# Squared queries split into two bf16 halves, reordered turns, double-buffered weight chunks, and an earlier context transpose in a gated cross-attention + ternary FFN kernel

## What is computed

```python
# x (32, 100, 512); ctx (32, 361, 256); 16 heads of 128; all fp32
h = layernorm(x)
q = rmsnorm((h @ Wq).reshape(B, 100, 16, 128), gq)
k = rmsnorm((ctx @ Wk).reshape(B, 361, 16, 128), gk)
v = (ctx @ Wv).reshape(B, 361, 16, 128)
a = softmax(einsum('bqhd,bkhd->bhqk', q, k) / sqrt(128))
x = x + tanh(g_xattn) * (einsum('bhqk,bkhd->bqhd', a, v).reshape(B, 100, 2048) @ Wo)
x = x + tanh(g_ffn) * bitlinear_ffn(layernorm(x))   # ternary weights, 8-bit activations, 512 -> 2048 -> 512
```

## Time and profile before

| | us |
|---|---|
| median of 3 runs | 2326.5 (2323.11 to 2329.4) |
| the profiled execution | 2321.96 |
| its span | 2320.2 |
| PE busy in the span | 2209.8 (95%) |
| DVE / ACT / POOL busy | 1820.5 / 1612.1 / 1265.4 |
| PE idle, 240 to 1080 us | 8.2 |
| PE idle, 1080 to 1920 us | 19.0 |

### The profile page before, as it was taken

How to read it: one execution, slowest core, us unless ns; L and a number is a source line. 1 busy time by engine, 2 the same in 40 slices (tenths; PEclk the granted TensorE clock), 3 DMA queues, 4 the chain that set the end, 5 groups by cost and what they waited for, 6 DMA issues and landing times. The chain is left out here.

```text
span 2320.2 us, 45840 instructions
## 1 busy us (share of the span) xinstructions
PE 2209.8 (95%) x16338; PEld 1564.2 (67%) x16338; DVE 1820.5 (78%) x4171; ACT 1612.1 (69%) x3398; POOL 1265.4 (55%) x1623
## 2 busy tenths in 40 slices
PE   5799999999999999999999999999999999769999
PEld 3567777777777777777777777776777777524444
DVE  5888877777877777877787787777877777579996
ACT  4677777777776777777777677776777677446665
POOL 4555656565656565656667676766676655200000
PEclk9999999999999999999999999999999999989999
DMA  6777676766767677657776767677767665635655
GB/s 147 172 152 141 127 143 127 141 135 129 141 129 143 130 140 128 136 105 149 136 146 135 154 132 154 132 146 136 137 145 139 132 108 115 177 87 142 140 139 125
DMA packets 921748, 317.53 MB, mean 137 GB/s; under 512 B 864912, under 2 KB 882608, under 8 KB 921264
## 3 DMA queue, kind: packets, MB, share of 16 engines
q1 hardware_dynamic: 921520, 314.61, 67.5%
HBM read 82.09 MB, written 19.40 MB: 44 GB/s over the span
## 5 line engine op out<-in xcount | busy, mean ns | idle before, releaser
L893 DVE TENSOR_TENSOR khat<-keys_ps,krs 128x512 f32<-128x512 f32 (+1 forms) x384 | 263.6, 686 | 286.2 <-POOL krs L1175 286.2
L1181 POOL TENSOR_TENSOR ksplit<-khat,ksplit 128x512 bf16<-128x512 f32 (+1 forms) x384 | 444.6, 1159 | 70.7 <-ACT ksplit L667 68.7
L1175 POOL TENSOR_TENSOR krs<-kvar,minus_half 128x4 f32<-128x4 f32 (+1 forms) x384 | 387.1, 1008 | 32.0
L689 ACT ACTIVATE prob<-score_ps,nbias,qrs 100x361 f32<-100x361 f32 x512 | 329.1, 647 | 65.3 <-DVE nbias L911 63.6
L1172 POOL TENSOR_SCALAR kvar<-kss 128x4 f32<-128x4 f32 (+1 forms) x384 | 88.6, 231 | 513.6 <-DVE kss L883 511.4
L672 ACT ACTIVATE ksq<-keys_ps 128x512 f32<-128x512 f32 (+1 forms) x384 | 228.3, 596 | 196.2 <-PE keys_ps L25 196.2
L923 DVE SCALAR_TENSOR_TENSOR psplit<-prob,rden,psplit 100x361 bf16<-100x361 f32 x512 | 349.3, 690 | 5.5 <-ACT psplit L698 1.4
L698 ACT ACTIVATE psplit<-prob,rden 100x361 bf16<-100x361 f32 x512 | 304.1, 594 | 49.6 <-DVE rden L917 48.7
L23 PE MATMUL keys_ps<-wk_split,ctxT 128*128 128x512 bf16 (+1 forms) x768 | 294.5, 383 | 26.2 <-DMA ctxT<-nat 14.7
L901 DVE TENSOR_REDUCE nmax<-score_ps 100x1 f32<-100x361 f32 x512 | 268.2, 524 | 54.6 <-PE score_ps L25 54.1
L667 ACT ACTIVATE ksplit<-khat 128x512 bf16<-128x512 f32 (+1 forms) x384 | 240.5, 626 | 85.0 <-DVE khat L893 83.7
(11 more groups left out here) (132 smaller groups left out, 5256.7 us busy)
## 6 DMA issues: line engine op xcount, KB each, us to landing
stage<-in_ffn SPq DMA_DIRECT2D x96, 256.0 KB, 3.2
ctx_raw<-in_ctx SPq DMA_DIRECT2D x31, 256.0 KB, 3.4
xin<-in_x SPq DMA_DIRECT2D x32, 200.0 KB
res_rows<-in_x SPq DMA_DIRECT2D x32, 200.0 KB
x_rows<-res_rows SPq DMA_DIRECT2D x32, 200.0 KB
xin<-x_rows SPq DMA_DIRECT2D x25, 256.0 KB, 2.8
xres<-x_rows SPq DMA_DIRECT2D x25, 256.0 KB, 3.0
out<-xres SPq DMA_DIRECT2D x25, 256.0 KB, 2.0
```

Source lines behind the costliest of these rows:

```text
L689: act.activation(prob[:, h, :], score_ps[h % 2][0:SQ, 0:SK], ACT.Exp, bias=nbias[:, b, h:h + 1], scale=qrs[:, v // 2 % 2, r:r + 1], accum_ ...
L893: dve.tensor_tensor(khat[0:KV[t], k, :].rearrange("p (h d) -> p h d", h=G), keys_ps[k][0:KV[t], :].rearrange("p (h d) -> p h d", h=G), rs, ...
L1175: pool.tensor_tensor(krs[0:KV[t], k, :], kvar[0:KV[t], k, :], minus_half[0:KV[t], 0:G], ALU.pow).then_inc(krs_done, 1)
L1181: pool.tensor_tensor(ksplit[0:KV[t], t, 1, :], khat[0:KV[t], (u + t) % 2, :], ksplit[0:KV[t], t, 0, :], ALU.subtract).then_inc(k_lo_done, 1)
```

## The change

- The squares are kept as two bf16 halves in one tile, `qsq_split`: ACT makes the fp32 squares (`queries_square`) of two heads and squares the same PSUM block a second time to bf16 (`queries_square_hi`), POOL subtracts (`query_squares_lo`). `query_squares` then issues 16 bf16 matmuls in place of 8 fp32 ones, with 128 columns of weights each (28 of them padding or a neighbour's), and stands later in PE's list, behind `heads_out` and the third key tile. `queries_lo` waits for both squares too.
- All four lists of `two_turns` have another order.
- Chunks have two buffers in and two out (`w_raw`, `w_out`, all in `stage`, which loses one of its seven load slots); the ternary part's load comes at the end of the turn before, the store one turn after the rounding.
- `ctx_raw` is filled earlier (turn 2 and turn 6 of the pair before), POOL splits it in turns 1 and 3 without a gap, and `turn_ctx` follows `turn_keys` in turns 4 and 5, where it stood ahead of `turn_keys` in turns 5 and 6.

The diff, cut to its core:

```diff
-    OWN_STAGES = 5
+    OWN_STAGES = 4
...
-        qsq = sb("qsq", [P, G, QT], F32)
+        qsq, qsq_split = sb("qsq", [P, TWO, QT], F32), sb("qsq_split", [P, 2 * G * QT + PAD], BF16)
...
-        w_raw, w_out = stage[:, 0, :], sb("w_out", [P, CHUNK], BF16)
+        w_raw, w_out = [stage[:, 0, :], stage[:, 3, :]], [
+            stage[:, 2, k * CHUNK // 2:(k + 1) * CHUNK // 2].bitcast(BF16) for k in range(2)]
...
             def query_squares(i, u):
...
-                eng.wait_ge(q_sq_done, i * (NG * QD) + ((u + 3) // 2 + 1) * QD)
+                eng.wait_ge(q_sqlo_done, i * (NG * QD) + ((u + 3) // 2 + 1) * QD)
                 for b in range(2):
                     for h in range(G):
-                        last = pe.matmul(ps[0:SQ, b * G + h:b * G + h + 1], qsq[:, h, b * SQ:(b + 1) * SQ],
-                                         ones[:, 0:1], start=True, stop=True)
+
+                        out, hi, lo = ps[:, b * G + h:b * G + h + 1], h * QT + b * SQ, (G + h) * QT + b * SQ
+                        pe.matmul(out, qsq_split[:, hi:hi + P], ones[:, 0:1], start=True, stop=False)
+                        last = pe.matmul(out, qsq_split[:, lo:lo + P], ones[:, 0:1], start=False, stop=True)
...
             def queries_square(i, u, k):
...
-                act.activation(qsq[:, k * TWO:(k + 1) * TWO, :],
-                               shared_ps[p][:, 0:TWO * QT].rearrange("p (h q) -> p h q", h=TWO),
-                               ACT.Square).then_inc(q_sq_done, 1)
+                if started(i * (NG * QD) + (u + 3) // 2 * QD + k):
+                    eng.wait_ge(q_sqlo_done, i * (NG * QD) + (u + 3) // 2 * QD + k)
+                act.activation(qsq[:, :, :], ps, ACT.Square).then_inc(q_sq_done, 1)
+
+            def queries_square_hi(i, u, k):
...
+                act.activation(qsq_hi[:, heads, :], ps, ACT.Square).then_inc(q_sqhi_done, 1)
...
+            def query_squares_lo(i, u, k):
...
+                pool.tensor_tensor(qsq_lo[:, heads, :], qsq[:, :, :], qsq_hi[:, heads, :],
+                                   ALU.subtract).then_inc(q_sqlo_done, 1)
```

PE's list in `two_turns` (the others change in the same manner):

```diff
                 if su:
-                    scores(i, u + 1, 0), scores(i, u + 1, 1)
+                    scores(i, u + 1, 0)
+                if qu:
+                    queries(i, u, 1)
                 if ku:
                     keys(i, u + 2, 2)
-                if qu:
-                    queries(i, u, 1)
                 if su:
-                    scores(i, u + 1, 2)
-                mixed(i, u, 0, par)
+                    scores(i, u + 1, 1), scores(i, u + 1, 2)
+                if kv:
+                    keys(i, v + 2, 0)
+                mixed(i, u, 0, par), mixed(i, u, 1, par)
                 if su:
                     scores(i, u + 1, 3)
-                if kv:
-                    keys(i, v + 2, 0)
-                mixed(i, u, 1, par)
                 if kv:
                     keys(i, v + 2, 1)
                 if new_x:
                     turn_x(i, 0)
-                if qu:
-                    query_squares(i, u)
-                if i == TERN_PAIR - 1 and u == 1:
-                    weight_totals(i)
                 heads_out(i, v, 0), heads_out(i, v, 1)
                 if new_x:
                     turn_x(i, 1)
                 if kv:
                     keys(i, v + 2, 2)
+                if qu:
+                    query_squares(i, u)
+                if i == TERN_PAIR - 1 and u == 1:
+                    weight_totals(i)
                 if sv:
                     scores(i, v + 1, 0), scores(i, v + 1, 1)
-                project(i, v, 0), project(i, v, 1)
+                project(i, v, 0), project(i, v, 1), project(i, v, 2), project(i, v, 3)
                 if sv:
-                    scores(i, v + 1, 2)
-                project(i, v, 2), project(i, v, 3)
-                if sv:
-                    scores(i, v + 1, 3)
+                    scores(i, v + 1, 2), scores(i, v + 1, 3)
```

More of the change, by code:

```diff
@@ L76, in shared_uses @@
             if more_queries(u, last):
-                order += [("q", u, 0)]
-            if more_queries(u, last):
-                order += [("q", u, 1)]
+                order += [("q", u, 0), ("q", u, 1)]
             order += [("m", u, 0), ("m", u, 1)]
@@ L82, in shared_uses @@
                 order += [("x", 0)]
-            if more_queries(u, last):
-                order += [("qss", u)]
             order += [("o", v, 0), ("o", v, 1)]
@@ L87, in shared_uses @@
                 order += [("x", 1)]
+            if more_queries(u, last):
+                order += [("qss", u)]
             if has_mixed(v, last):
@@ L386, in load_ternary @@
                 if u == 4:
-                    sp.wait_ge(w_tern_out, MATRICES * CHUNKS * 16)
+                    for k in range(2):
+                        sp.wait_ge(w_tern_out[k], MATRICES * CHUNKS // 2 * 16)
                     sp.wait_ge(shared_done, use(PAIRS - 1, ("q", UNITS - 5, QD - 1))[0] + 1)
@@ L406, in turn @@
                         load_x(i + 1, b, xin, x_in)
-                if not last and u == 3:
-                    sp.wait_ge(nat_ready, (i * 2 + 3) * KVT)
-                    load_ctx(i + 1, 1, ctx_raw)
-                if not last and u in (UNITS - 3, UNITS - 2):
-                    sp.wait_ge(keys_done, tile(i, u + 1, KVT - 1) + 1)
-                    turn_ctx(i + 1, u - (UNITS - 3), 1 - par)
                 if has_keys(u, last):
                     turn_keys(i, u + 2, 0), turn_keys(i, u + 2, 1), turn_keys(i, u + 2, 2)
+                if not last and u in (UNITS - 4, UNITS - 3):
+                    sp.wait_ge(keys_done, tile(i, u + 2, KVT - 1) + 1)
+                    turn_ctx(i + 1, u - (UNITS - 4), 1 - par)
                 load_pieces(i, u, 0)
@@ L421, in turn @@
                 load_pieces(i, u, 2)
+                if not last and u == 2:
+                    sp.wait_ge(nat_ready, (i * 2 + 3) * KVT)
+                    load_ctx(i + 1, 1, ctx_raw)
+                if i < PAIRS - 2 and u == UNITS - 2:
+                    sp.wait_ge(nat_ready, (i * 2 + 4) * KVT)
+                    load_ctx(i + 2, 0, ctx_raw)
                 store_chunk(i, u)
+                load_chunk(i, u, False)
                 if last:
@@ L1204, in split_ctx @@
                     eng.wait_ge(ctx_in[b], (j + 1) * 32)
-                    if not (isinstance(j, int) and j == 0):
-                        eng.wait_ge(shared_done, use(j - 1, ("m", 1, CC - 1))[0] + 1)
+                    if j > 1:
+                        eng.wait_ge(shared_done, use(j - 2, ("m", UNITS - 1, CC - 1))[0] + 1)
                 pool.tensor_copy(nat[0:KV[t], par, b, t, 0, :], raw[0:KV[t], t, :]).then_inc(nat_hi_done, 1)
```

271 lines of the change are left out of this document (156 added, 115 removed).

## The result

| | before | after |
|---|---|---|
| median of the runs, us | 2324.98 (2323.11 to 2329.4, 4 runs) | 2250.82 (2249.86 to 2254.29, 4 runs) |
| profiled execution | 2321.96 | 2254.29 |
| its span | 2320.2 | 2252.5 |
| first turn of `y` (end of pair 0) | 208.7 | 211.4 |
| last turn of `y` | 2030.4 | 1963.3 |

The ratio is 0.9681, 95% interval [0.9663, 0.9699]: 74 us faster, where 40 were forecast, and outside the range of 2262 to 2316.

What follows compares the result with a forecast made beforehand. PE was taken to bound the kernel, busy 2209.8 of 2320.2 us. Squares -36, waits that go -13, waits that come +6 and start +3 gave -40 us, from 2326.5 to 2287 us; range 2262 to 2316.

Steps and rivals of the forecast that it cites:

- The squares: PE's 64 square groups: a load-matmul pair falls from 84 to 49 ns, a group by 0.57 us; -36 us.
- rival C: The squares gain nothing: a fixed 84 ns per one-column matmul, or the chain waits as before; 2322 us, chance 0.09.
- Waits that go: PE's waits for PSUM banks: `qvar` -10, `qT_lo` -3, `xT_lo` and `khat` 0; sum -13 us.
- waits that come: Between second `mixed` and `heads_out`: less cover, so PE waits 0.1 us in each of 60 pairs of turns; +6 us.
- The clock: PE's granted clock was read as full nearly throughout, 2.4 GHz; the sum had no term for it.
- The tie: Ahead of `heads_out`: DVE's subtraction is ready after 1.73 us, against 1.75 us of PE's score and key tile.
- The context's transposes ahead of `turn_probs`: SP's queue in turn 5: three transposes, 4.83 us, covered by later-needed probabilities; 0, bounds 0 to 1 us in 15 pairs.
- The chunks' second buffers: Chunk loads and stores: second buffers take waits off SP's queue, not off PE; 0.
- Start +3: Kernel start: uncovered extra squares on ACT, subtractions on POOL and one load slot fewer; +3 us, ends 0 and 6.
- Drain 0: Kernel end: the 5.3 us wait for `pT` can go either way; 0, bounds ±5 us.
- Rival B: POOL's new subtraction delays DVE's `psplit`, reaching PE 0.86 us each two turns: +53, in sum +13; 2340 us, chance 0.09.
- Rival A: All 27 us of PE's steady idle and the drain's 5 vanish, squares at the skill's pace or better; 2262 us, chance 0.14.

Runs made afterwards that it cites:

- e3: The change with 100 weight columns in place of 128 for each bf16 square matmul; 2267.32 us.
- e1: The change with its squares back to eight fp32 matmuls a group, without ACT's second square and POOL's subtraction, new order kept; 2292.66 us.
- e2: The kernel before with the split bf16 squares alone, in the old order with one chunk buffer and old context turns; 2326.73 us.
- e12: The change's order with fp32 squares, these moved back to their old place ahead of `heads_out`; 2294.65 us.
- e6: The change with the second row's context transposes moved from turn 5 to the start of turn 6, ahead of `turn_keys`; 2242.37 us.
- e10: The change with one chunk buffer in and one out, loaded at a turn's start and stored in the same turn; 2348.06 us.
- e5: The change with POOL's subtraction of the query squares made twice each time; 2272.78 us.
- e9: The change with its bf16 squares, and DVE's reading of them, moved back ahead of `heads_out`; 2369.54 us.

## Why the prediction was wrong

The direction was right, and so was the main source, less work in the squares; its size was not, and a third source, the clock, was not in the sum. In the two profiled executions, whose difference is 67.7 us:

| term | forecast | measured |
|---|---|---|
| squares, PE's own work | -36 | -61, of it -53 in the 14 pairs |
| waits in the 14 pairs | -13 + 6 | -3 |
| lower clock in the 14 pairs | 0 | -11 |
| up to the first turn of `y`, with its squares | +3 | +2.7 |
| last pair and FFN, with their squares | 0 | -3 |

The other 6 us of the 74 are the places of the two profiled executions among their runs.

**The squares, forecast -36, measured -61 in PE's own work.** The step that failed is "I scale the pace by the shown load: 84 x 98/168 = 49 ns". The 64 groups fell by 0.95 us each. The measured pace is the shown load less 71 to 81 ns, so a scaling by ratio lies too high the shorter the load is. The 49 ns are nearly what the 100-column form of e3 takes (47), whose load shows 128 ns.
The Trainium skill (TensorE: Matmul & The Clock Gate, Weight-path perf modes and LDWEIGHTS) led to 53 ns as an estimate; the chip took 25, about half of that again, so the rule gives the direction of 128 columns against 100 here and not the size.
What my rival C said against the squares is decided too: there is no fixed cost of 84 ns.

**But 61 are not 42.** Put on top of the new order the squares brought 42, and in the old order nothing (e1, e2). The prediction took the squares' gain as if it came off the time whole. In the new order 1.0 us a pair more of waiting comes with the faster PE and the added work (1.63 to 2.64), 0.7 for `pT` and 0.3 for `kT`: 14 us, and 3 in the start. Which of the two brings it was not tried apart.

**Waits that go, forecast -13, and waits that come, +6: -7 in sum, and -3 in the change.** The reading of the waits was too low. By idle time they were 27 us; from the starts they are 2.82 x 14 = 39, since a modelled end hides up to 0.16 us of each. The new order alone (e1) takes 17 of these (2.82 to 1.63), with all of `qvar`; `khat`, put at 0, went as well (0.4 us a pair ahead of `keys`). The faster squares bring 14 back. `xT_lo`, put at 0 with bounds of 9, rose from 8.9 to 17.5 us, the upper bound.

**The clock, forecast 0, measured -11.** The step that failed is "its granted clock is full nearly throughout". The 0.99 of the earlier trace rows stands for seven stretches at 1.2 GHz, 24 us in all, in the steady pairs of before; the change and e1 have none (1.00 in the row below, from 240 to 1080 us). So 11 of the 28 us by which e1's 14 pairs are shorter than before's are no waits. All seven begin in a wait of PE or within 1.3 us behind one: five where, once a pair, the turned x and the squares come with waits of 0.26 and 0.47 us around the squares, two at the waits of 2.7 and 1.4 us for `qvar`. In e12, where the squares stand in their old place, there are five again, and the clock over the span is 0.984 or 0.985 in its four runs where e1 has 0.987 or 0.988. So the squares' place bears on whether the clock falls; why is not shown.

```profile
240.00:1080.00 840.00, 823.44 (x6688) 608.91 (x6745) 681.86 (x1607) 647.82 (x1483) 571.05 (x721) 1.00 0.74 138
```

The tie was real, and smaller: in the change's timeline of pair 7 DVE's second `uT` ends at 1020.75 and `heads_out` starts at 1020.90, 0.07 after its turn.

```profile
1020.19 0.56 DVE L906 TENSOR_TENSOR uT<-shared_ps,uT 128x400 bf16<-128x400 f32 x1
...
1020.62 0.38 PE L25 MATMUL keys_ps<-wk_split,ctxT 128*128 128x512 bf16 x1
...
1020.87 0.10 PEld L23 LDWEIGHTS shared_ps<-uT,wv_hi 128*128 128x128 bf16 x1 [0.37 <-DVE uT L906]
1020.90 0.25 PE L23 MATMUL shared_ps<-uT,wv_hi 128*128 128x200 bf16 x1
```

That is 1020.62 + 0.21 (a key matmul's step) = 1020.83 against 1020.90, in three of four places: 0.20 us a pair, 3 us for 6. It is as long in e1, so the faster squares do not add to it.

**The context's transposes ahead of `turn_probs`, forecast 0 with bounds of 0 to 1 us in each of 15 pairs**: 0.94 a pair, the upper end, of which e6 won 8.4 us back. "The probabilities have some 5 us more" was read from the pace of before. With the fp32 squares in the new order this wait is 0.23 a pair (e1); with the fast ones PE reaches `mixed` sooner and meets it in every pair.

**The chunks' second buffers, forecast 0**: against the kernel before this may stand, for SP waited little for the rounding there (11.6 us in 24 waits, 1080 to 1920 us). But the sum was made as if each part could be priced by itself. Without the buffers the new place of the rounding costs 97 us (e10), so they carry the order's gain.

**Start +3**: 2.7 measured, from the first turns of `y` (208.7 and 211.4), less what the squares of the start gain. **Drain 0**: the last pair and the FFN came out equal to within 3 us.

**Rival B** did not come: `psplit`'s mean fell from 690 to 646 ns, with 128 more operations on POOL; only when they are doubled does it come back to 688 (e5). The work of POOL is not free, though: e9 and e5 show PE waiting for its result by name. **Rival A** (2262) was nearest by luck: of the waits, which it let vanish, nearly all are left (2.82 to 2.64 a pair). The pace of the squares, better than it took, and the clock, which it did not have, stand in their place.

What stays open: how the 33 us of the order divide among its many moves. 11 are the clock in the profiled executions, and e12 shows that the squares' place gives nothing in sum; the reordered `mixed` and scores and the rounding's place were not tried alone.

## What to carry to other kernels

Read an almost saturated engine from its starts: each start to the next, less the median of its form. This gave PE's own work to 0.1 us a pair here, where idle time by modelled ends missed 12 of 39 us of waits. Then read the granted clock of the same stretches before calling late time a wait: 11 of 51 us were not. Before a step on the critical engine is made faster, ask what it covers; a gain of 61 us was worth 0 in the old order and 42 in the new one, and parts of such a change (a buffer, a place in a queue) have no price one by one.

## What the runs showed of the hardware

**Short bf16 matmuls go faster than their shown loads say.** A pair of a 128-column bf16 load and a one-column matmul follows the last at 25 ns, with 100 columns at 47, in fp32 with 100 at 88.

**The clock falls behind waits of PE, and not only behind long ones.** In e10, behind the wait of 2.8 us, the three matmuls of `scores` follow each other at 0.30 us (1540.64, 1540.94, 1541.24), in the change at 0.15. Busy times of e10 by stretch, with the granted clock in the third column from the end:

```profile
1536.00:1540.00 4.00, 1.49 (x18) 1.25 (x15) 1.28 (x2) 2.96 (x6) 2.04 (x4) 1.00 1.07 212
1540.00:1544.00 4.00, 3.69 (x23) 3.16 (x24) 2.40 (x5) 1.26 (x3) 1.85 (x4) 0.57 1.00 191
```

The clock was at 1.2 GHz for most of the 4 us after the wait. Of the 24 us that the low clock costs e10 in all, 16 lie in `queries` that waited for nothing. But in the kernel before it fell behind waits of 0.26 and 0.47 us with the fp32 squares between them (502 us, above), while the change's waits of about 1.2 us, once a pair for `xT_lo`, and of up to 1.75 for `pT` left it at 1.00. So the length of a wait alone does not tell; in before 24 us at 1.2 GHz cost 11 us, and they look like waits until the granted clock is read.
